# Cross-attention and mixture of experts on one core: the order of the last attention units' steps, one residual moved to GpSimd, one weight split moved to VectorE

## The chip, the cores and the metric

The kernel runs on 1 of the cores of a Trainium2 chip. The metric is device time in microseconds (us). The kernel before takes 631.37 us (median of 3 runs, 631.08 to 632.15). The engines are TensorE (PE, its weight loads PEld), VectorE (DVE), ScalarE (ACT), GpSimd (POOL) and SyncE (SP), which here only issues DMAs.

## The reference

Two steps with a residual each, on x of 4 x 512 x 512 in float32. N is the number of tokens, 2048.

```
x = x + xattn(layernorm(x), ctx, ctx)      # 8 heads of 64 rows, q and k l2-normalised per head,
                                            # scores times 5, softmax over keys, times v
x = x + ffn(layernorm(x))
ffn: logits = x @ Wg + bg                   # 4 experts, the best 2 of each token by logit, softmax over these 2
     for each expert: the 512 tokens with the highest probability for it (capacity N / 4)
         y = gelu(tok @ W1) @ W2 * p        # 512 -> 2048 -> 512, exact gelu
         out[these tokens] += y
```

In the attention, the second axis (512) of each batch is cut into 8 heads of 64 rows, and queries and keys are the 512 positions of the last axis.

## The kernel before

The attention is cut into 16 units of 128 rows (two heads each), numbered 0 to 15; in the code a unit is a pair `(h, parity)`, `end` is unit 15, `before(end)` unit 14. Each unit takes these steps: transposes and norms of queries and keys, scores on TensorE into the four banks `four`, exponentials on ScalarE (`prob`), half sums of them (`half_sum`, on VectorE), the weighted values into PSUM bank `two0` (`weighted_values`, L1270 to L1278) and the softmax sums into bank `two1` (`sums`, L1280 to L1289). ScalarE copies the values out (`take_o`, `o_sb`). For units 0 to 14 the sums are made small, inverted (`few_inv`) and spread again through DRAM by DMAs of SP (`spread_inverse`), which land in `p_inv`. For unit 15 VectorE inverts the whole bank directly (`invert_sums`, L848).

Behind that stand the steps of the second layernorm and of the router: `residual` (L858: `o_norm` = `o_sb` x `p_inv`, then `x_all` += `o_norm`, both of 128x512), `statistics_x2` (mean and variance), `finish` on GpSimd (the power -0.5, L512), `normalize_x2` (`x2n`), four transposes on TensorE (`transpose_x2`), a copy to `x2n_t` on ScalarE (`take_x2t`), eight small matmuls (`router_logits`) and an add on VectorE (`take_logits`). Units 12 to 15 run partly behind the attention's loop; there, the order on each engine is the order in which the code is written: L1006 to L1031 for VectorE, L566 to L573 for GpSimd, L722 to L743 for ScalarE, L1372 and what follows it for TensorE. An engine takes its instructions strictly in this order and waits for semaphores at their head.

Then come `keys_of` for the last four units, six rounds of a search for the threshold of each expert (VectorE and ScalarE count together: VectorE in `junk`, ScalarE by signs in `count_signs`), the slots of the tokens, and a one-hot matmul that finds which token lies in which slot (`slots_of`, which sets `idx_all`). With these indices GpSimd issues four indirect DMAs that gather the rows of expert 0 (`gather_x`, `x_got`, 128 rows each), and four more for the rows of the result (`o_got`). TensorE transposes each gathered tile, and starts with the first expert when the fourth is in. From there to the end TensorE is busy without a gap.

The experts' weights come in chunks of 1 MB, as two DMAs of 512 KB into one of two `raw` buffers. ScalarE rounds a chunk (`w_hi`), and `w_lo` = `raw` - `w_hi`. SP loads the next chunk into a buffer only when the `w_lo` of its last chunk is done (`wlo_done`, L464). The first two chunks are loaded and rounded early. Their `w_lo` is made by GpSimd, in quarters of 128x512 (`first_low`): three quarters of chunk 0 ahead of unit 15's `finish`, and the other five one per round, each held until the threshold of a round is set (`thr_done`). So chunk 2 is loaded after round 1, and chunk 3 after round 5. All later `w_lo` are made by VectorE (`split_lo`, one instruction of 128x2048).

## Time and profile before

| | |
|---|---|
| Time of 3 runs, median | 631.37 us |
| Profiled execution, its own device time | 629.77 us |
| Its span in the trace | 628.0 us |
| TensorE busy | 567.1 us (90%) |
| VectorE busy | 357.0 us (57%) |
| ScalarE busy | 281.6 us (45%) |
| GpSimd busy | 186.2 us (30%) |
| Mean granted clock of TensorE | 0.958 of full speed |

All times "at" a number are microseconds from the start of the span. In the page, the span is cut into 40 slices of 15.7 us. But for the start and the end, TensorE's busy tenths are 9 in all of them but three, slices 14 to 16 (204 to 251 us), where they are 5, 1 and 2; the granted clock there and in slice 17 is 7, 5, 5 and 6 tenths of full speed. This is the stretch between the attention and the experts. A step that ends earlier inside it can move all that follows; a step elsewhere lies beside a busy TensorE.

### The profile page before, as it was taken

The numbers are of one execution on the slowest core, as the hardware profiler recorded it, in microseconds if no ns is written. First come the engines' busy times: TensorE is split into PE (matmuls) and PEld (weight loads), VectorE is DVE, ScalarE is ACT, GpSimd is POOL, SyncE is SP. The second block draws the span as 40 slices with busy tenths as digits, with TensorE's granted clock in tenths as the row PEclk, the third lists the DMA queues.
The fourth block names the chain that finished last, engine by engine and source line by source line (L and its number), as shares of the span: only waits on it lengthen the run. The fifth ranks groups of instructions, "written<-read, shape, count | busy, mean of one in ns | idle before, by whom it ended". The sixth has DMA issues, their size and how long they took to land.

```text
span 628.0 us, 8727 instructions
## 1 busy us (share of the span) xinstructions
PE 567.1 (90%) x2842; PEld 407.4 (65%) x2842; DVE 357.0 (57%) x702; ACT 281.6 (45%) x421; POOL 186.2 (30%) x143
## 2 busy tenths in 40 slices
PE   1799999999999512999999999999999999999994
PEld 1445455455454401688888888888888788888883
DVE  4879899899988784534336443354543444424212
ACT  2587776776777240433243333433434324333320
POOL 4556656656642342200030330210420400500002
PEclk9999999999999755699999999999999999999998
DMA  5422332333312113332341543333452332442001
GB/s 144 159 96 85 118 132 89 117 123 95 102 69 94 75 67 103 99 134 68 134 134 68 183 151 134 100 100 110 157 179 88 117 120 97 172 163 68 0 1 67
DMA packets 46600, 67.73 MB, mean 108 GB/s; under 512 B 8560, under 2 KB 25072, under 8 KB 46576
## 3 DMA queue, kind: packets, MB, share of 16 engines
q1 hardware_dynamic: 42736, 54.84, 26.0%
q0 software_dynamic: 3840, 12.59, 6.0%
q8 instruction: 13, 0.21, 0.1%
q14 instruction: 11, 0.09, 0.1%
HBM read 54.70 MB, written 12.64 MB: 107 GB/s over the span
## 4 chain that ended last, share of the span: by engine, by line
PE 64%; DVE 5%; issue 4%; POOL 1%; DMA 1%; POOLq 0%; DVEq 0%; ACT 0%; SPq 0%
PE two L1423 29%; PE four L1453 9%; PE four L1452 9%; PE four L1450 9%; PE two L1276 2%; PE four L1266 2%; DVE junk L1045 1%; PE two L1288 1%; PE bank_t L1304 1%; DMA x_got<-x2n_dram,idx_all 1%; POOL w_lo L532 1%; DMA p_inv<-inv_dram 0%; PE bank_t L1411 0%; PE bank_m L1411 0%; DVE onehot L1132 0%
## 5 line engine op out<-in xcount | busy, mean ns | idle before, releaser
L758 ACT ACTIVATE h_f<-two 128x512 f32<-128x512 f32 x64 | 38.3, 599 | 231.4 <-PE two L1423 231.4
L1206 DVE TENSOR_TENSOR h_lo<-h_f,h_hi 128x512 fp32r<-128x512 f32 x64 | 44.1, 690 | 125.9 <-ACT h_hi L759 125.9
L1423 PE MATMUL two<-xt_hi,w_hi 128*128 (+1 forms) x256 | 102.9, 402 | 0.7 <-ACT xt_hi L747 0.7
L1423 PE MATMUL two<-xt_hi,w_lo 128*128 (+1 forms) x256 | 101.3, 396 | 0.0
L1423 PE MATMUL two<-xt_lo,w_hi 128*128 (+1 forms) x256 | 100.7, 396 | 0.0
L1453 PE MATMUL four<-w_hi,h_lo 128*128 128x512 f32 x256 | 100.5, 393 | 0.0
L1450 PE MATMUL four<-w_hi,h_hi 128*128 128x512 f32 x256 | 100.5, 392 | 0.0
L1452 PE MATMUL four<-w_lo,h_hi 128*128 128x512 f32 x256 | 100.4, 392 | 0.0
L652 ACT ACTIVATE prob<-four,rnorm 128x512 f32<-128x512 f32 x128 | 77.6, 688 | 25.3 <-POOL rnorm L476 18.2
L1176 DVE TENSOR_TENSOR w_lo<-raw,w_hi 128x2048 fp32r<-128x2048 f32 x30 | 68.7, 2291 | 23.3 <-ACT w_hi L685 23.3
L476 POOL TENSOR_TENSOR rnorm<-ss_max,power 128x8 f32<-128x8 f32 x32 | 64.6, 2018 | 49.6 <-DVE ss_max L807 48.3
L605 POOL DMA_INDIRECT out<-o_got,idx_all x16 | 20.2, 1264 | 165.4 <-DVE o_got L1227 163.0
L584 POOL DMA_INDIRECT x_got<-x2n_dram,idx_all x16 | 23.9, 1496 | 140.0 <-DVE idx_all L1163 125.3
L1276 PE MATMUL two<-prob,v_t 128*64 128x512 f32 x256 | 62.0, 605 | 0.0
L685 ACT ACTIVATE w_hi<-raw 128x2048 fp32r<-128x2048 f32 x32 | 61.3, 1918 | 0.0
L1423 PEld LDWEIGHTS two<-xt_hi,w_hi 128*128 128x128 f32 x256 | 48.6, 190 | 11.7 <-ACT xt_hi L747 1.1
L1423 PEld LDWEIGHTS two<-xt_hi,w_lo 128*128 128x128 f32 x256 | 48.6, 190 | 11.1
L1423 PEld LDWEIGHTS two<-xt_lo,w_hi 128*128 128x128 f32 x256 | 48.7, 190 | 10.7
L1453 PEld LDWEIGHTS four<-w_hi,h_lo 128*128 128x128 f32 x256 | 48.1, 188 | 10.8
L1450 PEld LDWEIGHTS four<-w_hi,h_hi 128*128 128x128 f32 x256 | 48.1, 188 | 10.8
L1452 PEld LDWEIGHTS four<-w_lo,h_hi 128*128 128x128 f32 x256 | 48.1, 188 | 10.7
L855 DVE TENSOR_TENSOR half_sum<-prob 128x512 f32<-128x512 f32 x64 | 41.5, 690 | 0.1
(174 smaller groups left out, 741.3 us busy)
## 6 DMA issues: line engine op xcount, KB each, us to landing
raw<-in_L_ffn_W SPq DMA_DIRECT2D x64, 512.0 KB, 4.0
x_all<-in_x SPq DMA_DIRECT2D x16, 256.0 KB, 2.7
c_sb<-in_ctx SPq DMA_DIRECT2D x16, 256.0 KB, 2.8
out<-x_all SPq DMA_DIRECT2D x16, 256.0 KB, 2.0
x2n_dram<-x2n SPq DMA_DIRECT2D x16, 256.0 KB, 2.0
p_inv<-inv_dram SPq DMA_DIRECT2D x30, 128.0 KB, 2.8
few<-p_sum SPq DMA_DIRECT2D x30, 2.0 KB, 2.2
cst<-in_consts SPq DMA_DIRECT2D x1, 354.5 KB, 4.2
```

Of the source, the lines that this page charges most:

```text
L476: return nc.gpsimd.tensor_tensor(dst, src, power[:, 0:n], ALU.pow)
L652: last = nc.scalar.activation(prob[h][t][:, :], s_ps[:, 2 * (t % 2) + h, :], ACT.Exp, scale=rnorm[u[1]][:, 0, t, h:h + 1])
L685: nc.scalar.activation(w_hi[c % SPLIT_BUFS][:, :], raw[c % RAW_BUFS][:, :], ACT.Copy).then_inc(whi_done, 1)
L758: nc.scalar.activation(h_f[m % 2][:, :], z_ps[m % 2][:, :], ACT.Gelu)
L855: nc.vector.tensor_tensor(half_sum[h][n][:, :], prob[h][2 * n][:, :], prob[h][2 * n + 1][:, :], ALU.add).then_inc(halves_done[h], 1)
L1176: nc.vector.tensor_tensor(w_lo[c % SPLIT_BUFS][:, :], raw[c % RAW_BUFS][:, :], w_hi[c % SPLIT_BUFS][:, :].bitcast(F32), ALU.subtract).then ...
L1206: nc.vector.tensor_tensor(h_lo[m % 2][:, :], h_f[m % 2][:, :], h_hi[m % 2][:, :].bitcast(F32), ALU.subtract).then_inc(h_split, 1)
L1276: last = nc.tensor.matmul(o_ps[0][DH * h:DH * (h + 1), :], v_t[u[1]][:, t, h, :], prob[h][t][:, :], start=(t == 0), stop=(t == TT - 1))
L1423: return nc.tensor.matmul(z[:, :], w_part[c][:, w], x_k, start=start, stop=stop)
L1450: nc.tensor.matmul(acc_ps[:, t, :], h_hi[m % 2][:, h], w_hi[c][:, w], start=(m == 0), stop=False)
L1452: nc.tensor.matmul(acc_ps[:, t, :], h_hi[m % 2][:, h], w_lo[c][:, w], start=False, stop=False)
L1453: last = nc.tensor.matmul(acc_ps[:, t, :], h_lo[m % 2][:, h], w_hi[c][:, w], start=False, stop=(m == MT - 1))
```

## The change

Six moves, no arithmetic is added or left out.

1. TensorE, unit 15: `sums` stands ahead of the weighted values of key tiles 2 and 3, not behind them.
2. VectorE: `invert_sums(end)` is the first step behind the loop. It stood behind unit 14's residual and statistics.
3. Unit 14's residual (two operations of 128x512) is GpSimd's, with `q_f` in place of `o_norm` as its scratch. VectorE's residual of unit 15 gets a wait for it and stands ahead of unit 14's `normalize_x2`.
4. GpSimd: the three quarters of `w_lo` between the two `finish` steps are gone. Chunk 0's four quarters wait for the thresholds 2 to 5.
5. Chunk 1's `w_lo` is made by VectorE in one `split_lo(0, 1)` of 128x2048, behind `slots_of(0)`, ahead of the `xt_lo` of the first expert.
6. ScalarE: `take_x2t` of unit 15 stands ahead of `count_signs(0)`, not behind it.

```diff
@@ GpSimd
+            def residual(u):
+
+                n = number(u)
+                xu = x_all[:, bass.ds(n, 1), :].rearrange("p a d -> p (a d)")
+                pool.wait_ge(o_taken, n + 1)
+                pool.wait_ge(inv_in, 32 * (n + 1))
+                pool.wait_ge(q_split, UNITS)
+                nc.gpsimd.tensor_tensor(q_f[:, :], o_sb[u[1]][:, :], p_inv[u[1]][:, :], ALU.mult).then_inc(on_done, 1)
+                pool.wait_ge(on_done, n + 1)
+                nc.gpsimd.tensor_tensor(xu, xu, q_f[:, :], ALU.add).then_inc(x2_done, 1)
...
+            residual((UNITS // 2 - 1, 0))
             finish((UNITS // 2 - 1, 0))
-            pool.wait_ge(sums_ready, UNITS)
-            for q in range(3):
+            finish((UNITS // 2 - 1, 1))
+            for q in range(4):
+                pool.wait_ge(thr_done, q + 2)
                 first_low(0, q)
-            finish((UNITS // 2 - 1, 1))
-            for q in range(3, 8):
-                pool.wait_ge(thr_done, q - 1)
-                first_low(q // 4, q % 4)
@@ ScalarE
             take_x2t((UNITS // 2 - 1, 0), bank_m)
+            take_x2t((UNITS // 2 - 1, 1))
...
             count_signs(0)
-            take_x2t((UNITS // 2 - 1, 1))
@@ VectorE, residual
                 if late:
+                    dve.wait_ge(x2_done, n)
                     dve.wait_ge(inv_done, late)
@@ VectorE, behind the loop
-            residual(before(end))
+            invert_sums(end)
             statistics_x2(before(end))
-            invert_sums(end)
+            residual(end, 1)
             normalize_x2(before(end), True)
             take_logits(before(before(end)))
-            residual(end, 1)
             statistics_x2(end)
@@ VectorE, behind slots_of(0)
+            dve.wait_ge(wlo_done, 1)
+            split_lo(0, 1)
             for t in range(ST):
@@ TensorE, unit
+                if not ahead:
+                    sums(u, behind, ahead)
                 weighted_values(u, 2)
                 weighted_values(u, 3)
-                sums(u, behind, ahead)
+                if ahead:
+                    sums(u, behind, ahead)
```

VectorE's queue behind the attention's loop, first as it is before. `p_inv<-two` is the inversion of unit 15's sums; the first `o_norm` belongs to unit 14, the second to unit 15.

```order
L1008 TENSOR_SCALAR thr<-cst 128x1
L867 TENSOR_TENSOR o_norm<-o_sb,p_inv 128x512
L869 TENSOR_TENSOR x_all<-x_all,o_norm 128x512
L876 MEMSET pad 128x1
L877 BN_STATS stats<-x_all 128x6
L879 MEMSET pad 128x1
L880 BN_AGGR mv<-stats 128x2
L882 TENSOR_SCALAR var_e<-mv 128x1
L848 RECIPROCAL p_inv<-two 128x512
L891 TENSOR_SCALAR x2n<-x_all,mv,rstd 128x512
L814 TENSOR_TENSOR logits<-bank_t,bgb 128x4
L867 TENSOR_TENSOR o_norm<-o_sb,p_inv 128x512
```

And as it is now (line numbers of the changed kernel):

```order
L1018 TENSOR_SCALAR thr<-cst 128x1
L857 RECIPROCAL p_inv<-two 128x512
L886 MEMSET pad 128x1
L887 BN_STATS stats<-x_all 128x6
L889 MEMSET pad 128x1
L890 BN_AGGR mv<-stats 128x2
L892 TENSOR_SCALAR var_e<-mv 128x1
L877 TENSOR_TENSOR o_norm<-o_sb,p_inv 128x512
L879 TENSOR_TENSOR x_all<-x_all,o_norm 128x512
L901 TENSOR_SCALAR x2n<-x_all,mv,rstd 128x512
L823 TENSOR_TENSOR logits<-bank_t,bgb 128x4
```

Unit 14's two residual operations have left VectorE, the inversion has moved from behind the statistics to the front, and the only residual left (unit 15's) stands ahead of unit 14's `x2n`.

GpSimd's queue from unit 14's last steps to the first gather, the difference of the two kernels. `rstd` is a `finish` step, `w_lo` a quarter of a chunk, `q_f` and `x_all` the moved residual.

```order
-L476 TENSOR_TENSOR rstd<-var_e,power 128x1 x3
-L532 TENSOR_TENSOR w_lo<-raw,w_hi 128x512 x3
-L476 TENSOR_TENSOR rstd<-var_e,power 128x1
-L532 TENSOR_TENSOR w_lo<-raw,w_hi 128x512 x5
```

```order
+L476 TENSOR_TENSOR rstd<-var_e,power 128x1 x2
+L519 TENSOR_TENSOR q_f<-o_sb,p_inv 128x512
+L521 TENSOR_TENSOR x_all<-x_all,q_f 128x512
+L476 TENSOR_TENSOR rstd<-var_e,power 128x1 x2
+L543 TENSOR_TENSOR w_lo<-raw,w_hi 128x512 x4
```

Eight quarters have become four, and the residual stands ahead of the last two `finish` steps.

VectorE's queue between the indices of expert 0 (`idx_all`) and the low parts of its gathered tokens, as it is now:

```order
L1161 TENSOR_SCALAR idx_all<-row 128x4
L1162 TENSOR_REDUCE prob_all<-four 128x4
L1185 TENSOR_TENSOR w_lo<-raw,w_hi 128x2048
L1204 TENSOR_TENSOR xt_lo<-bank_t,xt_hi 128x4x128
L1204 TENSOR_TENSOR xt_lo<-bank_m,xt_hi 128x4x128
```

Before, `xt_lo` followed on `prob_all` directly; the row with `w_lo` is new.

## Rows read from the trace of the kernel before

**Rows 1.** Chain of waits: start us, us, step.

```profile
215.24 1.10 PE bank_t L1296 x4
...
216.37 0.61 ACT x2n_t L678
...
217.01 1.88 PE bank_t L1304 x8
...
250.37 3.75 DMA x_got<-x2n_dram,idx_all
...
254.16 1.13 PE two L1411 x4
```

**Rows 2.** Timeline, VectorE: start us, us, instruction, idle before and releaser.

```profile
204.20 0.69 DVE L867 TENSOR_TENSOR o_norm<-o_sb,p_inv 128x512 f32<-128x512 f32 x1 [0.85 <-ACT o_sb L664]
...
206.68 3.35 DVE L848 RECIPROCAL p_inv<-two 128x512 f32<-128x512 f32 x1
...
209.94 1.41 DVE L891 TENSOR_SCALAR x2n<-x_all,mv,rstd 128x512 f32<-128x512 f32 x1
...
211.34 0.67 DVE L867 TENSOR_TENSOR o_norm<-o_sb,p_inv 128x512 f32<-128x512 f32 x1
...
212.05 0.69 DVE L869 TENSOR_TENSOR x_all<-x_all,o_norm 128x512 f32<-128x512 f32 x1
...
214.55 0.55 DVE L891 TENSOR_SCALAR x2n<-x_all,mv,rstd 128x512 f32<-128x512 f32 x1 [0.66 <-POOL rstd L476]
```

**Rows 3.** Timeline, TensorE.

```profile
201.13 1.94 PE L1276 MATMUL two<-prob,v_t 128*64 128x512 f32 x8
...
202.90 1.89 PE L1288 MATMUL two<-half_sum,cst 128*64 128x512 f32 x8
...
206.06 1.06 PE L1304 MATMUL bank_t<-wg,x2n_t 128*128 128x4 f32 x8 [0.69 <-ACT x2n_t L678]
...
211.40 0.66 PE L1296 MATMUL bank_m<-cst,x2n 128*128 128x128 f32 x4 [2.38 <-DVE x2n L891]
...
212.75 1.56 PE L1304 MATMUL bank_m<-wg,x2n_t 128*128 128x4 f32 x8 [0.69 <-ACT x2n_t L678]
```

**Rows 4.** Timeline, ScalarE and GpSimd.

```profile
212.59 1.11 ACT L733 ACTIVATE junk_a<-four,thr 128x1024 bf16<-128x1024 f32 x1
...
213.59 0.20 ACT L733 ACTIVATION_READ_ACCUMULATOR junk_a<-four,thr 128x1 f32 x1
...
207.35 3.71 POOL L532 TENSOR_TENSOR w_lo<-raw,w_hi 128x512 fp32r<-128x512 f32 x3
```

**Rows 5.** Windows: us, busy per engine, TensorE clock, DMA share, GB/s.

```profile
213.00:213.20 0.20, 0.20 (x4) 0.20 (x3) 0.20 (x1) 0.20 (x1) 0.00 (x0) 0.77 0.01 0
```

**Rows 6.** Timeline, VectorE, then GpSimd, at the first gather.

```profile
245.10 0.16 DVE L1153 TENSOR_REDUCE prob_all<-four 128x4 f32<-128x12 f32 x1
...
246.23 1.22 POOL L584 DMA_INDIRECT x_got<-x2n_dram,idx_all  x1 [11.05 <-issue]
...
250.37 1.00 POOL L584 DMA_INDIRECT x_got<-x2n_dram,idx_all  x1 [0.30 <-issue]
```

**Rows 7.** Timeline, VectorE, GpSimd and SyncE's queue, inside two experts.

```profile
317.33 2.29 DVE L1176 TENSOR_TENSOR w_lo<-raw,w_hi 128x2048 fp32r<-128x2048 f32 x1 [1.11 <-ACT w_hi L685]
...
317.40 3.10 POOL L584 DMA_INDIRECT x_got<-x2n_dram,idx_all  x1 [0.30 <-issue]
...
363.39 2.29 DVE L1176 TENSOR_TENSOR w_lo<-raw,w_hi 128x2048 fp32r<-128x2048 f32 x1 [1.11 <-ACT w_hi L685]
...
364.61 1.98 POOL L595 DMA_INDIRECT o_got<-out,idx_all  x1 [0.31 <-issue]
...
366.89 1.00 POOL L595 DMA_INDIRECT o_got<-out,idx_all  x1 [0.30 <-issue]
...
368.19 1.15 POOL L595 DMA_INDIRECT o_got<-out,idx_all  x1 [0.30 <-issue]
...
365.85 0.37 SPq L382 DMA_DIRECT2D raw<-in_L_ffn_W  x1
```

**Rows 8.** DMA issues at 250.37, 366.89 and 368.19: count, us to landing.

```profile
x_got<-x2n_dram,idx_all POOLq DMA_INDIRECT x1, 3.7
...
o_got<-out,idx_all POOLq DMA_INDIRECT x1, 5.4
...
o_got<-out,idx_all POOLq DMA_INDIRECT x1, 5.2
```

## The prediction

> **What bounds the kernel now.** I read the slices of the page first: TensorE is full except in three slices at 204 to 251 us. Whatever moves the end must end earlier or later in there. Then I read the chain of waits through that stretch. It runs over unit 15: x2n, its transposes at 215.24, the copy, the router's matmuls at 217.01 [rows 1], and from there through keys, six rounds and the slots, all serial on VectorE and TensorE, to the gather. It ends with the fourth indirect DMA at 250.37, whose 3.75 us hold back the last tile's transposes at 254.16 [rows 1]. Behind that TensorE has no gap. So the change has two ends to look at: when unit 15's logits come (front), and when the fourth gathered tile lands (back). A microsecond won or lost at either shows one to one in the time; between them nothing is changed but where GpSimd's quarters lie.
>
> **Front, VectorE's queue.** The timeline of VectorE shows the order that costs time: unit 14's residual 204.20, inversion 206.68 for 3.35, x2n of unit 14 209.94 for 1.41, unit 15's residual 211.34, its x2n at 214.55 for 0.55, so ready at 215.10 [rows 2]. From these rows: one operation of the residual and its gap takes 212.05 - 211.34 = 0.71, both 1.42. Residual and statistics of unit 14 take 206.68 - 204.20 = 2.48, so the statistics 1.06. From unit 15's residual to its x2n are 214.55 - 211.34 = 3.21, so GpSimd's power with both handovers is 3.21 - 2.48 = 0.73.
>
> Now the new order.
> - Inversion: TensorE's values at 201.13 and sums at 202.90 change places [rows 3]; the sums, 1.89 us, end at about 203.0. The half sums were ready before: the idle time in front of the sums is nil. VectorE is free at 204.20 - 0.85 = 203.35 [rows 2]. So the inversion runs 203.35 to 206.70. The values end at 204.8 instead of 203.1; the copy of them is wanted only at 208, so this costs nothing, and would cost something only if it came over 3 us later.
> - Unit 14's residual on GpSimd starts when its `p_inv` lands, 204.20 as before. A GpSimd operation of this size takes 3.71 / 3 = 1.24 [rows 4]; these three ran beside the inversion without either being longer, which is the same neighbour as in the new order. Two with a wait between: done at about 206.8. The multiply itself is not shown on GpSimd. Below: 0.69 as on VectorE, worth nothing, since the inversion ends at 206.7 anyway. Above: the two engines exclude each other, and both operations lie behind the inversion, done at 206.7 + 2.6 = 209.3. I take 206.8, the row nearest in size and engine.
> - Then VectorE: statistics of unit 14 206.9 to 207.95; unit 15's residual to 209.4 (the power of unit 14 is hidden by it); x2n of unit 14. That one took 1.41 while a GpSimd quarter ran and 0.55 alone [rows 2, 4]; no quarter runs now, so 209.95. A logits add of 0.1, statistics of unit 15 to 211.1, power 0.73, x2n to 212.4. Against 215.10: 2.7 us earlier.
>
> **Front, TensorE.** The next thing late is the router of unit 14. Its transposes began 0.05 after x2n and its matmuls 212.75 - 211.40 = 1.35 after them [rows 3]; now 210.0 and 211.35. At full clock the matmuls take 1.06 (206.06), at half clock 1.88, and 1.56 where the clock fell inside [rows 1, 3]. The row of the windows shows the fall: 0.77 in 213.0 to 213.2 [rows 5], after TensorE had been idle for 2.38 us before 211.40 and 0.69 before 212.75 [rows 3]. In the new order the first idle time is 1.4 shorter. I take the fall at the same place, 213.1: router of unit 14 full speed to 212.4, transposes of unit 15 from 212.45 (before 215.24) at full speed, 0.66 instead of 1.10, copy 0.61, router from 213.8 at half clock, to 215.7. Before: 217.01 + 1.88 = 218.9. So the front gives 3.2. If the clock is low from the start of these steps, the transposes of 14 take 0.44 more and its router ends at 213.7; unit 15 starts there, 1.5 earlier than before. If the clock stays high through unit 15's router, that ends at 214.9, but the signs are in the way: ScalarE now counts them behind unit 15's copy, 1.11 + 0.20 [rows 4], to 215.1, and VectorE's small step on them is ahead of the logits add: 3.7 at most. The front is 3.2, bounds 1.5 and 3.7. The move of the copy ahead of the signs is worth nothing by itself (they were through at 213.8, the copy came at 216.37); without it the signs would now lie in front of the copy and cost up to their 1.3 us.
>
> **Middle.** Chunk 0's quarters lie in rounds 1 to 4 where three of chunk 0's and chunk 1's lay; nobody waits for `w_lo` of chunk 0 before TensorE's first expert. Chunk 2 is then loaded after round 4, not 1, still some 15 us ahead of the gather. Nothing.
>
> **Back, the stall.** Chunk 1's `w_lo` on VectorE starts at 245.26, behind `prob_all` [rows 6], and by its form takes 2.29 [rows 7], to 247.55. VectorE had nothing to do there, so on VectorE it is free. But GpSimd starts its first indirect DMA at 246.23 and is through at 247.45 [rows 6], inside that time. Inside the experts the same pair is seen twice: w_lo 363.39 to 365.68 with an indirect DMA at 364.61 that takes 1.98, and 317.33 to 319.62 with one at 317.40 that takes 3.10, where one alone takes 1.00 [rows 6, 7]. Both end 0.9 after VectorE's instruction ends (366.59 and 320.50). So the first gather's issue ends at 247.55 + 0.9 = 248.45 instead of 247.45, and the other three follow in a row: +1.0. Bounds: 0 and 2.1 (3.10 - 1.00).
>
> **Back, the transfers.** SP may load chunk 3 only when chunk 1's `w_lo` is done: issued 0.17 after it, as at 365.85 [rows 7], so at 247.7 instead of 235.3 where no gather was near. Now 1 MB runs beside the 4 gathers. The trace has this nearly to the tenth, 118.15 us later: w_lo ends 365.68, raw issued 365.85, indirect issue ends 366.59, next ones at 366.89 and 368.19 [rows 7]. There the second took 5.4 to land and the third 5.2, where 3.7 is the rule with nothing beside [rows 8]. Carried over: second lands at 254.15, third at 255.25. The fourth has no counterpart; behind the third by the 1.1 that lie between these two, it lands at 256.3 at the latest. At the earliest it is unhindered, 251.37 + 3.7 = 255.1. By then most of the raw chunk has landed. I take 256.1; before, 250.37 + 3.7 = 254.1. So the back costs 2.0 in all, 1.0 of stall and 1.0 of sharing (bounds 0 and 1.3).
>
> **Sum.** -3.2 + 1.0 + 1.0 = -1.2 us. It is made on the profiled execution of 629.77; the runs' median, 631.37, is 1.6 above it, and the sum is taken from the median: 630.2. What a measurement can tell from no change is 0.2%, 1.26 us, so the forecast lies just inside "no change", and much hangs on terms of half a microsecond.
>
> **Rivals.**
> - One of the two back costs isn't paid: no stall, or the fourth gather is not slowed since the chunk is nearly in. -3.2 + 1.0 = -2.2, 629.2. For it: no row has this in the fourth gather, and the first stall depends on a lead of 1.3 us between two instructions. Against: two equal pairs. Chance 0.27, of which 0.1 is for no stall. No stall is what the first of the two rules of the Trainium skill above would give, and the time would be this one, 629.2.
> - TensorE's clock stays high through unit 15's router. -3.7 + 2.0 = -1.7, 629.7. For it: shorter idle times; against: a fall in the same place before. Chance 0.17.
> - Slower: GpSimd's residual and VectorE's inversion exclude each other, for both want the same part of the memory. Then unit 14's residual is done at 209.3 instead of 206.8, x2n of unit 15 at 214.9, and the front gives 0.2; with the back's 2.0 the sum is +1.8, 633.2. From 1.2 us of delay of the residual on, the change gains nothing; from 2.5 on, it is slower by what can be told. Against it: 3.71 and 3.35 beside each other [rows 2, 4]. Chance 0.06.
>
> **Chances and range.** The forecast has 0.50. Faster by over 0.2%: nearly all of the first rival, most of the second (0.14), and 0.06 of the forecast's own spread: 0.46. Slower by over 0.2%: 0.06. The rest, 0.48, is no change. The range: the low end is the first rival with some of the clock's gain, 628.9; the high end is a front of 1.9 with a back of 2.0 or one of 3.2 with the back at its bounds of 3.4, so 631.5. Left out above is the slower case.
>
> **What would show it.** In the profile of the changed kernel: the inversion starts near 203.4 and GpSimd's two operations of 1.24 end near 206.8 (later than 208: the third rival); unit 15's transposes near 212.5; logits of unit 15 near 215.8; the first indirect DMA takes some 2.2 instead of 1.22 (1.2: no stall); the raw pair is issued 0.2 behind `w_lo`; the fourth gather takes 4.7 to land, not 3.7; the last tile's transposes lie some 1.2 before 254.16. I would be wrong if anything between 216 and 245 changes its length, or if the experts, TensorE-bound before, show a wait for a chunk.

## The result: 0.4% faster, and the profile after

The changed kernel takes 628.36 us (median of 8 runs, 626.12 to 629.79) where the kernel before, run beside it, takes 630.82 (8 runs, 630.04 to 632.15). The ratio is 0.9957, 95% interval 0.9940 to 0.9975. A second set of runs on another occasion gave 0.9960 (0.9941 to 0.9979). Its medians, 629.08 against 630.33, lie only 1.25 apart, but its 11 runs are spread from 625.23 to 630.02, and their mean is 2.4 us below that of the kernel before. The ratios follow the means, so where medians and ratios differ, this text goes by the ratios. By them the change is worth 2.5 to 2.7 us. The prediction said 1.2 us, inside "no change", with a range from 628.9: the direction was right, the size was half of what was measured, and the time lies 0.5 below the range. It lies 1.8 below the forecast of 630.2. Of that 0.55 comes from the base, since the three runs shown before had a median of 631.37, not 630.82; the rest is in the terms. Taken from 630.82, the range would have begun at 628.35, at the measured time itself: the miss of the range is no larger than the error of the base, and the miss of the terms is what there is to learn from.

The page of the changed kernel, its span and the busy tenths of TensorE and its clock:

```profile
span 627.1 us, 8723 instructions
...
PE   1899999999999611999999999999999999999994
...
PEclk9999999999999855799999999999999999999998
```

The low stretch is nearly as deep as before: TensorE's tenths are 6, 1, 1 for 5, 1, 2 and those of its clock 8, 5, 5, 7 for 7, 5, 5, 6. The two profiled spans, 628.0 and 627.1, can't be compared directly: the attention's loop took longer in this execution. TensorE's router matmuls of unit 12 are the last work that the change leaves alone; they begin at 200.15 before and at 201.60 after. All distances below are therefore taken from that instruction, which I call the anchor.

VectorE's timeline of the changed kernel (start us, us, instruction, idle before and releaser):

```profile
205.20 3.35 DVE L857 RECIPROCAL p_inv<-two 128x512 f32<-128x512 f32 x1
...
208.70 0.69 DVE L887 BATCH_NORM_STATS2 stats<-x_all 128x6 f32<-128x512 f32 x1 [0.15 <-issue]
...
209.75 0.69 DVE L877 TENSOR_TENSOR o_norm<-o_sb,p_inv 128x512 f32<-128x512 f32 x1
...
211.09 0.54 DVE L901 TENSOR_SCALAR x2n<-x_all,mv,rstd 128x512 f32<-128x512 f32 x1
...
213.39 0.55 DVE L901 TENSOR_SCALAR x2n<-x_all,mv,rstd 128x512 f32<-128x512 f32 x1 [0.66 <-POOL rstd L476]
...
217.30 0.16 DVE L823 TENSOR_TENSOR logits<-bank_t,bgb 128x4 f32<-128x4 f32 x1 [0.60 <-PE bank_t L1315]
```

This answers [rows 2]. The inversion starts as soon as VectorE is free, and unit 14's statistics wait 0.15 us behind it, for GpSimd. Unit 14's x2n takes 0.54, not 1.41. Unit 15's x2n ends at 213.94, 12.34 behind the anchor; before it was 215.10, 14.95 behind it.

GpSimd's timeline: the moved residual, and the first indirect DMA.

```profile
206.04 1.27 POOL L519 TENSOR_TENSOR q_f<-o_sb,p_inv 128x512 f32<-128x512 f32 x1 [5.52 <-issue]
...
207.39 1.27 POOL L521 TENSOR_TENSOR x_all<-x_all,q_f 128x512 f32<-128x512 f32 x1
...
244.42 2.33 POOL L593 DMA_INDIRECT x_got<-x2n_dram,idx_all  x1 [13.46 <-issue]
```

The residual's two operations take 1.27 each beside the inversion, whose 3.35 is unchanged. The indirect DMA takes 2.33 where it took 1.22 [rows 6].

TensorE's timeline, same columns: the sums, unit 14's router, unit 15's transposes and router, the four gathered tiles, the first expert.

```profile
202.59 1.94 PE L1299 MATMUL two<-half_sum,cst 128*64 128x512 f32 x8
...
213.03 1.05 PE L1315 MATMUL bank_m<-wg,x2n_t 128*128 128x4 f32 x8 [0.69 <-ACT x2n_t L687]
...
214.08 0.63 PE L1307 MATMUL bank_t<-cst,x2n 128*128 128x128 f32 x4
...
215.39 1.87 PE L1315 MATMUL bank_t<-wg,x2n_t 128*128 128x4 f32 x8 [0.69 <-ACT x2n_t L687]
...
251.02 1.12 PE L1425 MATMUL bank_t<-cst,x_got 128*128 128x128 f32 x4 [8.05 <-DMA x_got<-x2n_dram,idx_all]
...
251.98 1.11 PE L1425 MATMUL bank_m<-cst,x_got 128*128 128x128 f32 x4
...
252.88 2.01 PE L1425 MATMUL two<-cst,x_got 128*128 128x128 f32 x8
...
255.58 0.79 PE L1437 MATMUL two<-xt_hi,w_hi 128*128 128x512 f32 x1 [0.69 <-ACT xt_hi L756]
```

Unit 14's router now runs at full clock from end to end (1.05, was 1.56 [rows 3]), and unit 15's transposes follow it without a gap, at 0.63 instead of the 1.10 of [rows 1]. The four tiles, each of which had its own wait before, run back to back.

For comparison three rows of the kernel before: the logits of unit 15, the indices, and the first matmul of the first expert.

```profile
218.92 0.16 DVE L814 TENSOR_TENSOR logits<-bank_t,bgb 128x4 f32<-128x4 f32 x1 [2.90 <-PE bank_t L1304]
...
245.02 0.17 DVE L1152 TENSOR_SCALAR idx_all<-row 128x4 uint32<-128x4 f32 x1
...
255.97 0.79 PE L1423 MATMUL two<-xt_hi,w_hi 128*128 128x512 f32 x1 [0.69 <-ACT xt_hi L747]
```

From these the account of the profiled executions, in us:

| stretch | before | after | difference |
|---|---|---|---|
| anchor to unit 15's logits | 18.77 | 15.70 | -3.07 |
| logits to `idx_all` | 26.10 | 25.90 | -0.20 |
| `idx_all` to the first expert | 10.95 | 12.38 | +1.43 |
| first expert to the end of the span | 372.03 | 371.52 | -0.51 |
| sum | | | -2.35 |

The sum is near the 2.5 to 2.7 of the runs. The start of the loop, 1.45 later after, is no part of the change.

### The profile page after: what moved, and what is told of

Read it like the earlier page. It is cut to its first block, busy times and chain, and to the rows that moved or that the text cites. A ratio compares the mean times of both kernels' runs of the same rounds, so it can differ in the third digit from the quotient of the medians.

```text
span 627.1 us, 8723 instructions
## 1 busy us (share of the span) xinstructions
PE 567.1 (90%) x2842; PEld 407.7 (65%) x2842; DVE 357.0 (57%) x701; ACT 281.7 (45%) x421; POOL 185.5 (30%) x141
## 4 chain that ended last, share of the span: by engine, by line
PE 65%; DVE 7%; DMA 2%; issue 2%; POOL 0%; ACT 0%; POOLq 0%; DVEq 0%; SPq 0%
PE two L1437 29%; PE four L1467 9%; PE four L1466 9%; PE four L1464 9%; PE two L1287 2%; PE four L1277 2%; DMA x_got<-x2n_dram,idx_all 1%; DVE junk L1054 1%; PE two L1299 1%; PE bank_t L1315 1%; PE bank_t L1425 1%; PE bank_m L1425 1%; DVE half_sum L864 1%; DVE p_inv L857 1%; DMA p_inv<-inv_dram 1%
## 5 line engine op out<-in xcount | busy, mean ns | idle before, releaser
L1185 DVE TENSOR_TENSOR w_lo<-raw,w_hi 128x2048 fp32r<-128x2048 f32 x31 | 71.0, 2290 | 23.3 <-ACT w_hi L694 23.3
L1437 PEld LDWEIGHTS two<-xt_hi,w_hi 128*128 128x128 f32 x256 | 48.6, 190 | 11.7 <-ACT xt_hi L756 1.1
L1437 PEld LDWEIGHTS two<-xt_hi,w_lo 128*128 128x128 f32 x256 | 48.6, 190 | 11.1
L1437 PEld LDWEIGHTS two<-xt_lo,w_hi 128*128 128x128 f32 x256 | 48.3, 189 | 10.6
L1466 PEld LDWEIGHTS four<-w_lo,h_hi 128*128 128x128 f32 x256 | 48.1, 188 | 10.6
```

The lines of the kernel that those rows point to most:

```text
L1185: nc.vector.tensor_tensor(w_lo[c % SPLIT_BUFS][:, :], raw[c % RAW_BUFS][:, :], w_hi[c % SPLIT_BUFS][:, :].bitcast(F32), ALU.subtract).then ...
L1437: return nc.tensor.matmul(z[:, :], w_part[c][:, w], x_k, start=start, stop=stop)
L1466: nc.tensor.matmul(acc_ps[:, t, :], h_hi[m % 2][:, h], w_lo[c][:, w], start=False, stop=False)
```

## The experiments

All ran beside the kernel before; ratios are to it, with 95% intervals. "Changed" is the changed kernel; times in profiles are from the anchor or from `idx_all`. The distance from `idx_all` to the last copy of a gathered tile (`xt_hi`) is the length of the back. It is 10.30 before and 11.73 in the changed kernel. Each profile is one execution, so a distance in it can differ from what is usual for its kernel.

**Chunk 1 back on GpSimd, two quarters a round.**

```diff
-            for q in range(4):
-                pool.wait_ge(thr_done, q + 2)
-                first_low(0, q)
+            for q in range(8):
+                pool.wait_ge(thr_done, q // 2 + 2)
+                first_low(q // 4, q % 4)
...
-            dve.wait_ge(wlo_done, 1)
-            split_lo(0, 1)
```

> The changed kernel, but chunk 1's low part goes back to GpSimd: eight quarters, two behind each of the thresholds 2 to 5, and VectorE's instruction behind slots_of(0) is gone. My theory: the change won about 3.1 us at the front (unit 15's logits), 0.2 in the rounds and 0.5 by an earlier full clock of TensorE, and lost 1.4 at the back through that instruction (stall of the first indirect DMA 1.1, rest the shared transfer). Then this kernel's first indirect DMA takes 1.2 instead of 2.33, from idx_all to the last xt_hi are 10.3 us instead of 11.7, and the time is 1.4 us (0.2%) below the changed kernel's and about 3.8 (0.6%) below the one before, near 627.0. Rival: the transposes of the four tiles bound the stage anyway (they ran back to back in the changed kernel), so the back costs nothing and the time is that of the changed kernel, -2.4. Second rival: pairs of quarters (2.5 us) do not fit in a round of 2.4 and slow VectorE's small steps; then the rounds are longer than 2.4 each and the time is above the changed kernel's.

631.50 us, ratio 1.0004 (0.9990 to 1.0018). The back is 10.40 long, as the theory says, but logits to `idx_all` grew from 25.90 to 29.78. The second rival holds: VectorE's small steps are slowed. VectorE's timeline and GpSimd's:

```profile
224.15 1.13 DVE L1057 SCALAR_TENSOR_TENSOR enough<-count,excess 128x1 bf16<-128x1 f32 x1
...
222.78 2.48 POOL L543 TENSOR_TENSOR w_lo<-raw,w_hi 128x512 fp32r<-128x512 f32 x2 [9.22 <-DVE thr L1087]
```

The small operation that ends a round's count reads two operands in SBUF; it takes 0.16 elsewhere and 1.13 here. GpSimd's pair ends at 225.26, VectorE's operation at 225.28. It looks like the stall of the gather with the roles changed: the second to come ends late. Four rounds of 0.97 make the 3.9. One quarter of 1.26 ends before the count does, and so costs nothing; that is what had hidden GpSimd's quarters. By the ratio the run ends where the kernel before does, since the 3.9 take back what the front and the back give.

**The back alone, on the kernel before.**

```diff
-            for q in range(3, 8):
-                pool.wait_ge(thr_done, q - 1)
-                first_low(q // 4, q % 4)
+            pool.wait_ge(thr_done, 2)
+            first_low(0, 3)
...
+            dve.wait_ge(wlo_done, 1)
+            split_lo(0, 1)
             for t in range(ST):
```

> The kernel before with edit 5 alone: chunk 1's low part by VectorE behind slots_of(0); GpSimd makes only chunk 0's fourth quarter behind threshold 2. Nothing at the front changes. My theory: idx_all to the last xt_hi grows from 10.3 to 11.7, so the time is 1.4 us (0.2%) above the kernel before, less up to 0.5 if TensorE reaches its full clock earlier relative to the first expert, as in the changed kernel. The prediction's terms say +2.0. Rival, the back costs nothing since the transposes bound it: +0.0.

632.14 us, ratio 1.0022 (1.0005 to 1.0039): slower by 1.4 us by the ratio. In its profile the back is 13.70 long, 3.4 more than before, not 1.4. The indirect DMA took 2.32, so the stall is the same 1.1; the sharing is 2.3 here and 0.3 to 0.4 in the changed kernel. But this execution is not the usual one: it took 633.37, 1.2 above the median of its 12 runs, although its attention's loop was the shortest of all the profiles (anchor at 200.01). The ratio allows 1.4 us for the whole edit, so 2.3 of sharing is what one execution paid, and the usual price here is probably lower. That the time rises at all shows that the transposes don't hide the back.

**The stall alone.**

```diff
                     sp.wait_ge(wlo_done, e * CHUNKS + c + 1)
+                    if c == 1:
+                        sp.wait_ge(x_gathered[ST - 1], 16 * (e + 1))
```

> The changed kernel, but SP issues chunk 3 only when the fourth x_got gather has landed. The stall of the first indirect DMA stays (2.3 us instead of 1.2), the transfer beside the gathers is gone. My theory, back = stall 1.1 + sharing 0.4: idx_all to the last xt_hi 11.3, the time 0.4 us below the changed kernel's. The prediction had 1.0 each: 1.0 below. Chunk 3 lands near 259, before ScalarE wants it (268), so its lateness costs nothing; if it did, TensorE would wait for z or w_lo in the first expert.

628.15 us, ratio 0.9961 (0.9947 to 0.9976). The back is 11.58: stall +1.28, and with the load beside it 0.15 more. In time that is no difference to the changed kernel. So by this pair the load costs the changed kernel next to nothing. No wait for chunk 3 appeared.

**The split behind the tiles.**

```diff
-            dve.wait_ge(wlo_done, 1)
-            split_lo(0, 1)
             for t in range(ST):
                 dve.wait_ge(xthi_done, t + 1)
...
+            dve.wait_ge(wlo_done, 1)
+            split_lo(0, 1)
             for e in range(1, E):
                 payload(e)
```

> The changed kernel with split_lo(0, 1) moved behind the four xt_lo instead of ahead of them. Neither stall nor sharing at the x_got gathers; the two last o_got issues of GpSimd may be held back, which nobody waits for soon. My theory: as the kernel with the pairs on GpSimd, idx_all to the last xt_hi 10.3 and the time 1.4 us below the changed kernel's, about 627.0. Rival: chunk 1 is late for TensorE's third block (m = 2), then PE waits on w_lo early in the first expert and part of it is lost; by the trace that block starts some 9 us behind xt_hi, so I expect none.

627.18 us, ratio 0.9942 (0.9926 to 0.9957). The back is 10.39, the first indirect DMA 1.24. By the ratios it is about 1 us better than the changed kernel, where 1.4 was expected. The back is 1.34 shorter, as expected, and the front 0.5, but the clock came back 5.2 us into the first expert, and from there to the end it took 0.6 more. It is the best order of the kernel's own steps that was run.

**The load alone beside the gathers, on the kernel before.**

```diff
                     sp.wait_ge(wlo_done, e * CHUNKS + c + 1)
+                    if c == 1:
+                        sp.wait_ge(dummy_done, 2)
...
+            for n in range(2):
+                nc.vector.tensor_scalar(junk[:, :], four_flat[:, SIGNS:], thr[:, 0:1], None,
+                                        ALU.is_ge, ALU.add, accum_out=count[:, :]).then_inc(dummy_done, 1)
+                dve.wait_ge(dummy_done, n + 1)
             for t in range(ST):
```

> The kernel before, but chunk 3's load is put off until VectorE has run two extra counts (2.6 us, one operand in PSUM and none other in SBUF) behind slots_of(0); their result is used by nobody. So the load lies beside the x_got gathers as in the changed kernel, without the stall: GpSimd's first indirect DMA should take 1.2, not 2.3. What it tells apart: in the profile of the changed kernel idx_all to the last xt_hi is 11.7, in that of the kernel before with the split on VectorE 13.7, with the stall alone 11.6, with neither 10.3 to 10.4. If sharing is what varies, this kernel shows 10.5 to 12.6 there and spreads more from run to run than the kernel before; the median some 0.5 to 1.5 us above it. If the load never costs anything by itself, it shows 10.3 and +0.0.

634.22 us, ratio 1.0052 (1.0035 to 1.0069), the slowest of all; more than the upper value expected. GpSimd's, SyncE's and TensorE's timelines:

```profile
246.50 1.22 POOL L587 DMA_INDIRECT x_got<-x2n_dram,idx_all  x1 [11.08 <-issue]
...
248.27 0.37 SPq L383 DMA_DIRECT2D raw<-in_L_ffn_W  x1
...
250.16 1.12 PE L1418 MATMUL bank_t<-cst,x_got 128*128 128x128 f32 x4 [5.13 <-DMA x_got<-x2n_dram,idx_all]
...
255.49 1.12 PE L1418 MATMUL bank_m<-cst,x_got 128*128 128x128 f32 x4 [4.21 <-DMA x_got<-x2n_dram,idx_all]
```

No stall: 1.22, and the first tile comes at 4.9 behind `idx_all` as before. The second comes 5.3 us later, where 1.4 was the rule. The back is 13.83. Here the profiled execution, 633.69, is near the median, and the ratio says 3.3 us. So sharing alone can cost 3.5 us, 3.5 times the term of the prediction, and stall and sharing don't add up: with both, the back alone, it was at most 3.4.

**The sums late again.**

```diff
-                if not ahead:
-                    sums(u, behind, ahead)
                 weighted_values(u, 2)
                 weighted_values(u, 3)
-                if ahead:
-                    sums(u, behind, ahead)
+                sums(u, behind, ahead)
```

> The changed kernel with the first edit undone: unit 15's sums stand again behind the weighted values. By the rows the sums end 1.8 later, VectorE's inversion starts 1.4 to 1.5 us later than the time it is free at, ends that much later, and covers GpSimd's residual; logits of unit 15 come some 1.3 later. If the time follows: 1.3 us (0.2%) above the changed kernel's. Rival: the inversion is hidden by the wait for unit 14's p_inv anyway, then 0.0.

629.14 us, ratio 0.9971 (0.9957 to 0.9984), 0.7 to 0.9 us above the changed kernel's two ratios. In the profile the inversion starts at least 1.1 later from the anchor (4.69, where the profiles with the new order have 3.07 to 3.60) and the logits come at 16.81, where they have 15.1 to 15.7. Its interval and that of the changed kernel overlap, so the profile carries this reading, not the time. This execution's first expert ran at full clock from its first matmul, and took 369.74 to the end of the span instead of 371.52: 1.8 us by the clock alone, which hid the 1.1.

**The residual on VectorE again.**

```diff
             invert_sums(end)
+            residual(before(end))
             statistics_x2(before(end))
...
-            residual((UNITS // 2 - 1, 0))
```

> The changed kernel with the third edit undone: unit 14's residual is VectorE's again, behind the inversion. Two operations of 0.71 come between the inversion and unit 14's statistics, less the 0.15 that VectorE waited for GpSimd: logits of unit 15 1.2 to 1.3 later, time 1.2 us above the changed kernel's. If GpSimd's residual slowed the inversion, that would be 3.35 here as well or shorter; I expect 3.35 in both.

630.55 us, ratio 0.9987 (0.9968 to 1.0006). VectorE's timeline:

```profile
203.81 3.35 DVE L856 RECIPROCAL p_inv<-two 128x512 f32<-128x512 f32 x1
...
207.08 0.63 DVE L875 TENSOR_TENSOR o_norm<-o_sb,p_inv 128x512 f32<-128x512 f32 x1
...
208.48 0.69 DVE L885 BATCH_NORM_STATS2 stats<-x_all 128x6 f32<-128x512 f32 x1
```

The inversion takes 3.35 with and without GpSimd beside it. The statistics start 4.67 behind the inversion instead of 3.50, so 1.2 later, as expected, and unit 15's x2n follows 1.1 later behind the inversion's start. The logits come at 17.06, 1.4 later than in the changed kernel; the inversion began 0.5 earlier from the anchor in this execution, and unit 14's router and unit 15's transposes ran partly or wholly at half clock, which took 0.7. So by the profile this move gives about as much as that of the sums, 1.1; by the ratios it gives more, 1.7 to 1.9 us.

**The signs ahead of the copy again.**

```diff
             take_x2t((UNITS // 2 - 1, 0), bank_m)
-            take_x2t((UNITS // 2 - 1, 1))
...
             count_signs(0)
+            take_x2t((UNITS // 2 - 1, 1))
```

> The changed kernel with the sixth edit undone: ScalarE counts the signs of round 0 ahead of unit 15's copy. The prediction said that they would now lie in front of the copy and cost up to 1.3 us. By the profile of the changed kernel ScalarE is idle for 1.77 us ahead of that copy, more than the 1.31 of the signs, so they fit: unit 15's logits where they are in the changed kernel, VectorE's step on the signs earlier, time that of the changed kernel within 0.1%. If the prediction's bound is right, the logits come up to 1.3 later.

629.04 us, ratio 0.9968 (0.9954 to 0.9982); the changed kernel in the same call 0.9960. ScalarE's timeline and TensorE's:

```profile
212.30 1.11 ACT L742 ACTIVATE junk_a<-four,thr 128x1024 bf16<-128x1024 f32 x1
...
213.29 0.20 ACT L742 ACTIVATION_READ_ACCUMULATOR junk_a<-four,thr 128x1 f32 x1
...
215.31 0.60 ACT L687 ACTIVATE x2n_t<-bank_t 128x512 f32<-128x512 f32 x1 [1.81 <-PE bank_t L1307]
...
212.45 1.87 PE L1315 MATMUL bank_m<-wg,x2n_t 128*128 128x4 f32 x8 [0.69 <-ACT x2n_t L687]
...
214.18 1.09 PE L1307 MATMUL bank_t<-cst,x2n 128*128 128x128 f32 x4
```

ScalarE still waits 1.81 us for TensorE behind the signs. TensorE was slow in this execution, but the changed kernel's own row agrees: at full clock ScalarE was idle for 1.77 us ahead of that copy, more than the 1.31 of the signs.

```profile
214.74 0.60 ACT L687 ACTIVATE x2n_t<-bank_t 128x512 f32<-128x512 f32 x1 [1.77 <-PE bank_t L1307]
```

So the sixth edit is worth nothing, and the prediction's up to 1.3 for its absence was wrong. The logits did come at 16.60, 0.9 later than in the changed kernel, by another cause: in this execution the clock was low from unit 14's transposes on (1.11, was 0.66), so for its router (1.87, was 1.05) and unit 15's transposes (1.09, was 0.63).

**Chunk 2's load late as well.** Against the back alone:

```diff
-            pool.wait_ge(thr_done, 2)
+            pool.wait_ge(thr_done, 5)
             first_low(0, 3)
```

> The kernel before with the split of chunk 1 on VectorE (as in the run with the back alone), but chunk 0's fourth quarter behind threshold 5 instead of 2, so that chunk 2 is loaded 12 us ahead of idx_all as in the changed kernel, not 19. Seen so far: idx_all to the last xt_hi takes 11.7 in the three profiles with the changed kernel's loads (raw at -12, +2.6) and 13.7 and 13.8 in the two with chunk 2 at -19 and chunk 3 at +2.6 or +3.0. If the time of chunk 2's load decides, this run shows 11.7 and is 1.5 to 2 us faster than the run with the back alone; if it is something else in the front, it shows 13.7.

631.97 us, ratio 1.0027 (1.0014 to 1.0040), like the back alone. The back is 12.90, between the two values. With one profile each, this shows that the time of chunk 2's load is not the whole cause; whether the 0.8 between 13.70 and 12.90 is its share or chance stays open.

**The changed kernel again,** without an edit.

> The changed kernel once more, on the same chip and in the same call as three of its variants. By its first profile: logits of unit 15 3.1 us earlier than before by TensorE's own time, idx_all to the last xt_hi 11.7, ratio to the kernel before 0.996. What may differ is the place at which TensorE's clock comes back in the first expert (3.8 us into it there, 5.0 before): if that was luck of one execution, it is 4.8 to 5.2 here.

629.08 us, ratio 0.9960 (0.9941 to 0.9979). Logits at 15.47, the back 11.75, clock back 4.0 into the first expert. All three terms repeat within 0.3.

**TensorE kept busy in the wait.** On the split behind the tiles:

```diff
+            def warm(calls):
+
+                for _ in range(calls):
+                    nc.tensor.matmul(two[1][:, :], cst[:, C_ONES:C_ONES + P], cst[:, 0:512], start=True, stop=True)
...
+            warm(4)
             find(0, four[:, 0, :])
+            warm(5)
```

> The changed kernel with split_lo(0, 1) behind the xt_lo (as in the run before of that name), and nine float32 matmuls of 128x512 on constants that nobody reads: four ahead of the one-hot matmuls of expert 0, five behind them, where TensorE waits for the gather. Theory: in all kernels so far the granted clock is at its lower level until 3.8 to 5.2 us into the first expert, because TensorE had been nearly idle since unit 15's router; matmuls at half clock take 0.43 instead of 0.23. If the clock is up when the tiles come, four transposes and 5 us of matmuls run at full speed: 2.5 to 3.0 us saved, time near 624.5, 1% below the kernel before. Rival: the added matmuls are too few or too early, the clock is low again by the first tile and nothing is saved. Third: they reach into the gather's landing and delay the first tile; it shows as idle_all to the first transposes above 4.8.

626.05 us, ratio 0.9927 (0.9905 to 0.9948): 1 us of the 2.5 to 3.0 expected. The windows (us, busy of PE, PEld, DVE, ACT, POOL, then TensorE's clock, DMA share, GB/s) show why:

```profile
251.00:252.00 1.00, 0.63 (x4) 0.39 (x4) 0.63 (x1) 0.33 (x1) 0.81 (x1) 1.00 0.84 234
...
252.40:253.00 0.60, 0.60 (x2) 0.50 (x3) 0.60 (x2) 0.60 (x1) 0.51 (x1) 0.50 0.57 219
...
255.60:256.40 0.80, 0.80 (x5) 0.66 (x4) 0.77 (x3) 0.00 (x0) 0.00 (x0) 1.00 0.13 42
```

The clock is up when the tiles come, and falls as the expert begins, behind tiles between which TensorE was idle 0.7 to 0.8 us each. It comes back 3.2 us into the expert.

**And between the tiles.** As before, with 6 calls behind `find`, and one behind each tile, into a bank that is free (`warm` now takes the bank as an argument):

```diff
                 transpose_tokens(t, (bank_t, bank_m, *two)[t])
+                warm(1 if t < ST - 1 else 1, four[:, 3, :])
```

> As the run with nine added matmuls, with one more behind the one-hot matmuls and one behind each of the four tiles' transposes, written to a free bank. In that run the clock was up from before the tiles, but fell again as the first expert began and came back 3.2 us into it, since TensorE stood idle 0.7 to 0.8 us between tiles. Theory: with the gaps filled it doesn't fall, the first 3.4 us of the expert run at 0.23 per matmul instead of 0.43: 1.5 us less than that run, 624.5, 1% below the kernel before. Rival: the fillers delay the tiles' transposes by as much as they save (each takes 0.5 at full clock, 1.0 at half).

623.35 us, ratio 0.9892 (0.9871 to 0.9912), the best of all: 7 us below the kernel before, and by the ratios about 3 us below the split behind the tiles (0.9942). TensorE's timeline:

```profile
247.67 0.60 PE L1430 MATMUL bank_t<-cst,x_got 128*128 128x128 f32 x4
...
248.11 1.02 PE L1413 MATMUL four<-cst 128*128 128x512 f32 x2
...
252.11 0.66 PE L1430 MATMUL two<-cst,x_got 128*128 128x128 f32 x4
...
253.45 0.50 PE L1442 MATMUL two<-xt_hi,w_hi 128*128 128x512 f32 x1
...
253.79 0.40 PE L1442 MATMUL two<-xt_hi,w_lo 128*128 128x512 f32 x1
```

The expert's matmuls take 0.40 from the second on (starts 0.23 apart), where they took 0.63 (0.43 apart) for about 4 us. The first expert to the end of the span is 369.75.

## Why the prediction was half of what was measured

**Front, right.** The prediction said 3.2, measured is 3.07 in the first pair of profiles. Over all with the same order, the logits come 15.1 to 15.7 behind the anchor in the new order (seven profiles, 15.36 in the mean) and 18.55 to 18.8 in the old (four, 18.68 in the mean), so 3.3 apart. By steps: inversion free of the wait, yes (3.60 behind the anchor, 203.35 would be 3.20; this execution's loop left VectorE later); GpSimd's two operations 1.27 each for 1.24; the handover and the statistics 0.15 behind the inversion; x2n of unit 14 0.54 for 0.55; unit 15's x2n 2.6 earlier for 2.7; the transposes at full clock and the router of unit 15 at half, as taken. The rival in which the two engines exclude each other is excluded by two inversions of 3.35, with GpSimd beside it and without, and by GpSimd's 1.27 beside it. What the prediction took as a value is a draw, though: where the clock falls. In the run with the signs first it fell earlier and took 0.9 of the front, inside the bounds of 1.5 and 3.7.

**Sixth edit, half right.** That it is worth nothing was said; that its absence would now cost up to 1.3 was wrong, by ScalarE's idle 1.77 ahead of the copy.

**Stall, right.** +1.0 forecast. The indirect DMA took 2.33 for 1.22, +1.1, and ended 1.11 behind VectorE's operation (0.9 was carried over). VectorE's rows and SyncE's, changed kernel:

```profile
243.20 0.17 DVE L1161 TENSOR_SCALAR idx_all<-row 128x4 uint32<-128x4 f32 x1
...
243.36 2.28 DVE L1185 TENSOR_TENSOR w_lo<-raw,w_hi 128x2048 fp32r<-128x2048 f32 x1
...
245.80 0.37 SPq L382 DMA_DIRECT2D raw<-in_L_ffn_W  x1
```

The split ends at 245.64, the indirect DMA at 246.75. The Trainium skill's page SBUF — State Buffer, section "Who interferes with whom", infers that `tensor_tensor` doesn't hold descriptor generation. Here and in each run with the split in that place it held it back by 1.1 us (2.30 to 2.34 in eight profiles), and the runs without the split there show 1.22 to 1.24. With the Trainium skill's other rule in that place, that a two-input operation contends with a GpSimd instruction that reads SBUF, the traces agree, and the pairs of quarters show it from the other side. Which access of the indirect DMA is held back, no run shows.

**Sharing, the term that was mis-sized: this step failed.** The step said that the fourth gather lands at 256.1, 11.1 behind `idx_all`, 1.0 of it by sharing. The four gathers of the changed kernel, count and us to landing:

```profile
x_got<-x2n_dram,idx_all POOLq DMA_INDIRECT x1, 6.5
...
x_got<-x2n_dram,idx_all POOLq DMA_INDIRECT x1, 4.9
...
x_got<-x2n_dram,idx_all POOLq DMA_INDIRECT x1, 4.2
...
x_got<-x2n_dram,idx_all POOLq DMA_INDIRECT x1, 4.1
```

The fourth is issued at 249.68 and lands at 253.8, 10.6 behind `idx_all`. It was 9.05 before, so the back costs 1.5, and 1.43 at the first expert: 0.3 to 0.4 of sharing for 1.0, and 0.15 by the run with the stall alone. I carried the second and third landing over from a place inside an expert and added a spacing of 1.1 for the fourth. The carried 5.4 and 5.2 for the second and third came out as 4.9 and 4.2. In the changed kernel the first gather suffers most (6.5 for 3.5, of which 1.1 is the stall), the fourth least (4.1 for 3.7). But it would be wrong to call 0.4 the price: in its one profile each, the same load cost 2.3 with the same stall on the kernel before, 1.5 in its variant, 3.5 without a stall. Five profiles with the changed kernel's front, or most of it, and the load beside the gathers showed backs of 11.7 to 11.9, three with the front of before 12.9 to 13.8. SP issued the load 2.6 us behind `idx_all` in all of them but the one without a stall (3.0), so its place doesn't explain it. What does, the runs don't show; the time of chunk 2's load was tried and is at most a part of it. For the changed kernel 0.4 lies inside the prediction's bounds (0 to 1.3); as the price of such a load they were too narrow upwards.

**The first expert's clock, a term that was missing.** Windows with the return of the full clock, changed kernel, then before:

```profile
259.40:259.60 0.20, 0.20 (x2) 0.16 (x2) 0.00 (x0) 0.00 (x0) 0.00 (x0) 0.99 0.00 0
```

```profile
260.80:261.20 0.40, 0.40 (x3) 0.33 (x2) 0.00 (x0) 0.00 (x0) 0.00 (x0) 0.88 0.00 0
```

It came back 3.8 us into the first expert, for 4.9 before, and 4.0 in the repeat. The stretch from there to the end is 0.5 shorter for it. The prediction held that behind 254.16 everything only shifts. It doesn't: the clock's return moves against the start of the expert. That activity in the wait can move it is shown by the two runs with added matmuls. In the changed kernel the delayed tiles ran back to back, 3.9 us without a gap, directly ahead of the expert, and it is tempting to call this the cause. The other profiles don't bear it out. With the tiles apart the clock came back 4.7 to 5.2 us into the expert (four profiles). With two or more of them back to back it came back after 3.7 to 4.0 in three, but after 4.8 to 5.2 in four others, among them the run with the signs first, whose tiles lay like the changed kernel's. The run with the sums late had it up before the expert began. So the 0.5 is partly or wholly luck of the executions, and its cause stays open.

**The middle,** 0.2 for 0. It is the same in all kernels of either kind: 26.09 to 26.11 with the front of before and with the residual on VectorE, 25.90 to 25.93 in the others but the one with pairs. All of it lies in one place, the step that sets the last threshold. Of the changed kernel, then of the kernel before:

```profile
231.80 0.21 DVE L1097 TENSOR_SCALAR thr<-cst,low 128x1 f32<-128x1 f32 x1
```

```profile
233.62 0.21 DVE L1088 TENSOR_SCALAR thr<-cst,low 128x1 f32<-128x1 f32 x1 [0.21 <-DVE low L1085]
```

With the old order, and with the residual on VectorE, this step waits 0.21 for VectorE's own step ahead of it, and in the changed kernel it doesn't. Why, the runs don't show. The prediction had named any change of this stretch as a sign of being wrong; it came, at 0.2.

Together: front -3.07 for -3.2, middle -0.20 for 0, back +1.43 for +2.0, clock -0.51 for 0. Of the 1.15 us that the sum missed, 0.6 is the back, all of it the sharing priced at 1.0, and 0.5 the clock, a term put at nothing without a reason; the front and the middle nearly cancel.

## What to carry to other kernels

A slot in which one engine is idle is free only if the instruction put there holds back no neighbour and releases nothing that does: VectorE's idle 6 us were the gather's issue and the gather's bandwidth, and the same instruction behind the four tiles left the back at 10.39, for 10.30. VectorE's operations with two operands in SBUF and GpSimd's work were seen to hold each other back in both directions: the one that came second ended with the other (0.16 became 1.13) or 1.1 behind it (1.22 became 2.33). What counts is whether the first ends before the critical one starts. Ahead of a long TensorE-bound part, matmuls that nobody reads, placed in the wait up to its very end, can be worth about as much as the reordering: here some 3 us on top of the 3.7 of the better order.

## What the runs showed of the hardware

- A load of 1 MB beside four indirect gathers of 256 KB cost between 0.15 and 3.5 us on the last of them, in kernels that differ elsewhere, one profile each.
- A VectorE operation on 128x1 with both operands in SBUF took 1.13 us for 0.16, until GpSimd's 2.48 us of two operations ended.
- With nine added matmuls in the wait TensorE's granted clock was at its upper level when the tiles came, and fell again in spite of transposes of 0.66 each 1.4 us; with one filler more between them it stayed up. Full clock from the first matmul of the expert on makes it 369.7 us to the end (two profiles), where it is 371.3 to 372.4 in the others.
- From execution to execution most kernels spread by 3 to 6 us, and the profiles differ among themselves in the length of the attention's loop (anchor at 200.0 to 202.4) and in the place of the clock's fall and return. A change of 1 us at the front shows in the profile, taken from an anchor, better than in medians of 12 runs; at the back one profile can mislead, as the back alone shows.
